# Output projection of heads 0 to 13 by seven block products per pair of heads instead of eight, from batch 2 on

## The reference

```
x = x + attention(layernorm(x))
x = x + ffn(layernorm(x))
# attention, head h:
#   scores = (q_nope k_nope^T + rope(q_pe) rope(k_pe)^T) / sqrt(192);  p = softmax(scores)
#   out   += (p v_h) @ wo_h^T          (512 x 128 times 128 x 512, for each head)
# ffn: silu(x Wg * sg) * (x Wu * su), then @ Wd * sd, weights rounded to fp8
```

## Time and profile before

| | |
|---|---|
| time, median of 3 runs | 2230.44 us (2229.0 to 2231.82) |
| profiled execution, from first to last instruction | 2228.8 us |
| PE busy | 2205.4 us, 10977 matmuls |
| DVE, ACT, POOL busy | 1557.8, 1066.6, 1001.5 us |
| chain that ended last | 93% PE, 3% DVE |
| granted TensorE clock | 0.999 of full speed, mean |
| DMA, all from SP's queue | 218 MB, 47.7% of 16 engines |

### The profile page before, as it was taken

The page is one execution under the profiler, slowest core; times in us unless marked ns, Lnnn a source line. Parts: engine busy times, 40 slices in busy tenths (PEclk is TensorE's granted clock), DMA queues, the critical chain, the costliest instruction groups (busy, mean ns, idle before and its releaser), DMA issues.

```text
span 2228.8 us, 34908 instructions
## 1 busy us (share of the span) xinstructions
PE 2205.4 (99%) x10977; PEld 1026.8 (46%) x10977; DVE 1557.8 (70%) x3227; ACT 1066.6 (48%) x2345; POOL 1001.5 (45%) x688
## 2 busy tenths in 40 slices
PE   7999999999999999999999999999999999999999
PEld 5444544445444454444544445444454445444454
DVE  7888887776477764777648775587755877467773
ACT  6667564554255542555325553355443554345532
POOL 4657465453355524454244642536334363343322
PEclk9999999999999999999999999999999999999999
DMA  7868336562175631756216561365614564145530
GB/s 248 188 124 150 88 71 142 106 124 51 23 151 105 122 53 34 145 105 127 44 43 146 106 121 29 73 123 106 118 25 104 106 115 95 24 104 109 106 65 19
DMA packets 703800, 219.42 MB, mean 98 GB/s; under 512 B 685520, under 2 KB 685776, under 8 KB 702672
## 3 DMA queue, kind: packets, MB, share of 16 engines
q1 hardware_dynamic: 703696, 218.09, 47.7%
HBM read 40.78 MB, written 8.39 MB: 22 GB/s over the span
## 4 chain that ended last, share of the span: by engine, by line
PE 93%; DVE 3%; ACT 1%; DMA 1%; POOL 1%; issue 1%; SPq 0%; DVEq 0%; POOLq 0%
PE bank L853 13%; PE bank L291 11%; PE bank L293 11%; PE bank L292 11%; PE scores L863 7%; PE scores L663 5%; PE scores L293 5%; PE scores L291 5%; PE scores L292 5%; PE bank L674 4%; PE bank L675 4%; PE bank L676 4%; PE scores L660 3%; PE bank L840 1%; PE bank L689 1%; PE scores L557 1%
## 5 line engine op out<-in xcount | busy, mean ns | idle before, releaser
L1716 POOL TENSOR_TENSOR arena<-arena 128x1024 f16<-128x1024 f32 x256 | 545.7, 2132 | 620.3 <-ACT arena L1079 620.3
L1077 ACT ACTIVATE arena<-scores,shift 128x512 f32<-128x512 f32 x512 | 357.5, 698 | 535.0 <-DVE shift L1429 494.8
L1449 DVE SCALAR_TENSOR_TENSOR arena<-bank,rden,arena 128x512 f32<-128x512 f32 x508 | 347.9, 743 | 137.0 <-PE bank L293 137.0
L1427 DVE TENSOR_REDUCE mx<-scores 128x1 f32<-128x512 f32 x512 | 352.5, 689 | 20.5 <-PE scores L293 16.7
L1079 ACT ACTIVATE arena<-scores,shift 128x512 f16<-128x512 f32 x512 | 358.6, 700 | 0.0
L853 PE MATMUL bank<-arena,WFF 128*128 128x512 f16 x1392 | 313.5, 379 | 0.8 <-DVE arena L1601 0.6
L1774 POOL TENSOR_TENSOR arena<-arena 128x512 f16<-128x512 f32 x96 | 114.4, 1191 | 255.6 <-ACT arena L1152 255.6
L853 PEld LDWEIGHTS bank<-arena,WFF 128*128 128x128 f16 x1392 | 135.9, 98 | 164.1 <-DVE arena L1601 2.3
L291 PE MATMUL bank<-WVO,arena 128*128 (+1 forms) x512 | 194.2, 379 | 2.4 <-DVE arena L1222 1.2
L1222 DVE SCALAR_TENSOR_TENSOR arena<-bank,arena 128x512 f16<-128x512 f32 (+1 forms) x263 | 176.2, 670 | 29.1 <-ACT arena L1070 24.4
L663 PE MATMUL scores<-arena 128*128 128x512 f16 x512 | 195.4, 382 | 0.0
(11 more groups left out here) (159 smaller groups left out, 3480.5 us busy)
## 6 DMA issues: line engine op xcount, KB each, us to landing
arena<-arena SPq DMA_TRANSPOSE x712, 3.2
arena<-w_ffn SPq DMA_DIRECT2D x24, 384.0 KB, 3.5
arena<-x SPq DMA_DIRECT2D x8, 1024.0 KB, 5.6
out<-arena SPq DMA_DIRECT2D x32, 256.0 KB, 2.0
arena<-x SPq DMA_DIRECT2D x14, 512.0 KB, 4.4
WVO<-w_o SPq DMA_DIRECT2D x4, 1024.0 KB, 8.2
arena<-w_nope SPq DMA_DIRECT2D x4, 768.0 KB, 9.1
arena<-down_scale SPq DMA_DIRECT2D x8, 256.0 KB, 3.3
```

The source lines that it names most:

```text
L1077: act.activation(P32[:, t, :], SC[:, t, :], ACT.Exp, scale=EXP_SCALE, bias=shift[:, t:t + 1], accum_out=esum[:, par, t:t + 1]).then_inc(s[ ...
L1427: dve.tensor_reduce(mx[:, t:t + 1], SC[:, t, :], AX_X, ALU.max).then_inc(s["mxr"], 1)
L1449: dve.scalar_tensor_tensor(out=XR[:, t, :], in0=banks[t][:, :], scalar=by[:, t:t + 1], in1=XR[:, t, :], op0=ALU.mult, op1=ALU.add).then_in ...
L1716: pool.tensor_tensor(PL[:, par, two, :], P32[:, two, :], PH[:, par, two, :], ALU.subtract).then_inc(s["pl"], 1)
```

## The change

From batch 2 on, the outputs of heads 2j and 2j+1 (j = 0 to 6) are made together. Both contexts side by side are 512 rows by 256, both weights one above the other 256 by 512. Cut in two by two blocks, this product is made with seven block products in place of eight (Winograd's form of Strassen's scheme), from sums and differences of the context's blocks (`E1, O1, O2, S1..S4`) and of the weights' blocks (`B11, B21, B22, T1..T4`). A block product (`duo_product`) is two row tiles x three matmuls of 256 columns. The sums of weights are made once, in batch 1, by POOL and ACT in the place of the weights, and stored to DRAM (`w_duo`); from batch 2 on they are streamed in for each pair, in an early and a late part, into one buffer. The sums of contexts are made on POOL for each pair. Since products mix heads, the context must be scaled by the softmax reciprocal before: a row of 512 reciprocals is written to DRAM and read back broadcast to all partitions, and DVE multiplies the context by it. Heads 14 and 15, and batches 0 and 1, keep the old form. The loops over pairs in PE and ACT are written out in the new batches.

```diff
+EARLY = [(X_E1, W_B11, 0, True), (X_S1, W_T1, 1, True), (X_O1, W_B21, 2, True), (X_S2, W_T2, 0, False)]
+LATE = [(X_S3, W_T3, 0, False), (X_S4, W_B22, 1, False), (X_O2, W_T4, 2, True)]
+ADDS = [(0, 0, 0), (1, 1, 1), (2, 0, 0), (0, 0, 1), (0, 1, 0), (0, 1, 1), (1, 0, 1), (2, 1, 0)]
+        DBANK = (BO, BT, BC)
 # SP
+            def early_blocks(b, j):
+                if j == 0:
+                    sp.wait_ge(s["t_out"], 16 * N_DUO)
+                    sp.wait_ge(s["outp"], b * (NH * NT))
+                else:
+                    sp.wait_ge(s["outp"], b * (NH * NT) + 8 * (j - 1) + N_EARLY)
+                sp.dma_start(WB[:, :, 0:N_EARLY], w_duo[j, :, :, 0:N_EARLY]).then_inc(s["w_early"], 16)
+            def row_of_head(b, i):
+                sp.wait_ge(s["rden"], b * NH + i + 1)
+                sp.dma_start(rows_d[i % 2].rearrange("(t p) -> p t", p=P), rden_duo[:, i % 2],
+                             allow_slow_non_contiguous=True).then_inc(s["row_out"], 16)
+                sp.wait_ge(s["row_out"], (b - B_PLAIN) * (16 * 2 * N_DUO) + 16 * (i + 1))
+                sp.dma_start(ROW[:, i % 2], rows_d[i % 2:i % 2 + 1].broadcast_to((P, S))).then_inc(row_in[i % 2], 16)
...
                     head(i, base, i % 2, ahead=i < NH - 2, first=first)
+                    if not plain:
+                        if i < 2 * N_DUO:
+                            row_of_head(b, i)
+                        if i == 0:
+                            early_blocks(b, 0)
+                            late_blocks(b, 0)
+                        elif i >= 4 and i % 2 == 0:
+                            early_blocks(b, i // 2 - 1)
+                        elif i >= 5:
+                            late_blocks(b, i // 2 - 1)
...
 # PE
+            def duo_product(j, x, w, k, start):
+                for t in range(2):
+                    dst = DBANK[k][:, t * HB:(t + 1) * HB]
+                    for m, (p, q) in enumerate(((0, 0), (0, 1), (1, 0))):
+                        r = pe.matmul(dst, lhsT=XP[j % 2][:, p, x, tile(t)], rhs=WB[:, q, w, :],
+                                      start=(start and t == 0 and m == 0), stop=(m == 2), skip_group_check=True)
+            def duo_early(b, j):
+                n, base = (b - B_PLAIN) * N_DUO + j + 1, b * (NH * NT) + 8 * j
+                pe.wait_ge(s["w_early"], 16 * n)
...
+                    if x == X_S1:
+                        pe.wait_ge(s["x_lo"], n)
+                    if x == X_O1:
+                        pe.wait_ge(s["cth"], b * N_CT + min(2 * j + 3, 2 * N_DUO))
+                    if x == X_S2:
+                        pe.wait_ge(s["outr"], base + 1)
+                    duo_product(j, x, w, bk, start).then_inc(s["outp"], 1)
+            def duo_step(b, i, ahead=True):
+                scores(b, pair, par)
+                values(b, *before(pair, par))
+                if ahead:
+                    absorb(i + 2, b * NH + i + 2)
+                if i >= 3 and i % 2:
+                    duo_early(b, (i - 3) // 2)
+                elif i >= 4:
+                    duo_late(b, (i - 4) // 2)
 # ACT
+            def sum_hi(j):                     # batch 1, 128 x 1024
+            def context_hi(b, i):
+                act.wait_ge(s["cth"], b * N_CT + i + 1)
...
+            def duo_step(b, i):
+                probs(b * NH + i, i % 2, False)
+                context_hi(b, i - 1)
+                qa_hi(b * NH + i + 2, i % 2)
 # DVE
+            def duo_step(b, i, part=None):
+                maxima(g)
+                if part in (0, 1, 2):
+                    next_norm(b, part)
+                context_by_row(b, i - 1)
+                row_of_sums(b, i)
+                qa_lo(g + 2, i % 2)
+                context_lo(b, i - 1)
+                if part in (2, 3):
+                    next_norm(b, part + 1)
+                duo_adds(b, i)
 # POOL: block_sums in batch 1: ten tensor_tensor of 128 x 256; block_sums_lo: one of 128 x 1024
+            def context_sums(b, j):
+                step(x[X_S1], x[X_S3], x[X_O2], ALU.add, 0)
+                step(x[X_S3], x[X_E1], x[X_S3], ALU.subtract, 1)
+                step(x[X_S2], x[X_S1], x[X_E1], ALU.subtract, 0)
+                step(x[X_S4], x[X_O1], x[X_S2], ALU.subtract, 3)
+                pool.tensor_copy(XP[j % 2][:, 0, X_S3:], X32[:, X_S3:]).then_inc(s["x_sum"], 1)
+                pool.tensor_tensor(XP[j % 2][:, 1, X_S3:], X32[:, X_S3:], XP[j % 2][:, 0, X_S3:],
+                                   ALU.subtract).then_inc(s["x_lo"], 1)
...
                     head(base + i, i % 2)
+                    if not plain and i >= 2 and i % 2 == 0:
+                        context_sums(b, i // 2 - 1)
+                    if plain and not first and i >= 2:
+                        if i % 2 == 0:
+                            block_sums(i // 2 - 1)
+                        else:
+                            block_sums_lo(i // 2 - 1)
```

More of the change, by code:

```diff
@@ L464, in batch @@
                         weight_chunk(chunk_of(i) + 2)
+                if plain and not first:
+                    sums_of_blocks(N_DUO - 1)
                 sp.wait_ge(s["ctp"], (b + 1) * N_CT)
@@ L511, in _ @@
             output_matrix(3)
-            batch(0, False, first=True)
-            with sp.Fori(1, B - 1) as b:
+            batch(0, False, first=True, plain=True)
+            batch(1, False, plain=True)
+            with sp.Fori(B_PLAIN, B - 1) as b:
                 batch(b, False)
@@ L776, in attention @@
                     rotated_ahead(b, n)
-                head_step(b, 0, 1)
-                if first:
+                if b >= B_PLAIN:
+                    for i in range(1, NH - 2):
+                        duo_step(b, i)
+                else:
+                    head_step(b, 0, 1)
+                if b >= B_PLAIN:
+                    pass
+                elif first:
                     for i in range(2, NH - 2):
@@ L1112, in attention @@
                         head_step(i, base, i % 2, chunk=chunk_of(i), weights=True)
-                else:
[L1114 to L1117, removed]
+                elif plain:
+                    for i in range(2, NH - 2):
+                        head_step(i, base, i % 2)
+                        if i >= 3 and i % 2:
+                            sum_hi((i - 3) // 2)
+                else:
+                    for i in range(2, NH - 2):
+                        duo_step(b, i)
                 for k in range(2):
@@ L1181, in ffn, with batch @@
                     qa_hi((b + 1) * NH + 1, 1)
-            def batch(b, last, first=False):
-                attention(b, last, first)
+            def batch(b, last, first=False, plain=False):
+                attention(b, last, first, plain)
                 ffn(b, last, first)
@@ L1212, in _ @@
             setup_queries_and_keys()
-            batch(0, False, first=True)
-            with act.Fori(1, B - 1) as b:
+            batch(0, False, first=True, plain=True)
+            batch(1, False, plain=True)
+            with act.Fori(B_PLAIN, B - 1) as b:
                 batch(b, False)
@@ L1565, in last_of_attention @@
                 maxima(g)
-                for t in range(NT):
+                if b >= B_PLAIN:
+                    duo_adds(b, NH - 1)
+                for t in range(NT if b < B_PLAIN else 0):
                     add_out(g - 2, t)
@@ L1746, in attention @@
+            def attention(b, last, first, plain):
                 base = b * NH
@@ L1802, in _ @@
             rotate(0, NT)
-            batch(0, False, first=True)
-            with pool.Fori(1, B - 1) as b:
+            batch(0, False, first=True, plain=True)
+            batch(1, False, plain=True)
+            with pool.Fori(B_PLAIN, B - 1) as b:
                 batch(b, False)
```

218 lines of the change are left out of this document (200 added, 18 removed).

## The result

The changed kernel takes 3054.0 us (median; 3051.4 to 3055.0) against 2231.1 of the kernel before (2229.0 to 2234.5) on the same chip: ratio 1.3685, 95% interval 1.3666 to 1.3704. The forecast was 2294, range 2250 to 2350. The direction was right, the time is far outside the range.

A forecast was written before the change was run, and what follows sets the result against it. It took TensorE, 99% busy and 93% of the last-ending chain, as the bound. Batches 2 to 6 lose 10.0 each (50), batch 7 6.1, batch 1 8: +64 on 2230.4 gives 2294, range 2250 to 2350.

The forecast's parts named there:

- The row of reciprocals: Each head's write to DRAM and broadcast back from SP: write lands in 2.6, costing nothing at 2.0 to 3.7.
- the rows' round trip is the bound: Rival: chain from SP over two DMAs to PE bounds, from a write of about 3.7 us; 2385 at 5; chance 0.25.
- 256-wide products: PE: 42 matmuls of 256 columns per pair at 0.109 replace 24 of 512; saves 0.58 per pair, 24.4 us in all.
- wait for DVE's first add: PE's fourth early product waits for DVE's first add: 0.7 in first pair, then 1.5 a pair, 8.2 per batch.
- DVE's low halves of the context: DVE's low context half ahead of the adds: 0.7 in the even step, 0.42 in the odd step.
- weights' place: Early weights on SP's queue land near +8.7 of the odd step; up to 1.3 later costs nothing.
- POOL, batches 2 to 6: POOL's context sums and normalisation make it 3.6 late at step 9, PE waits 1.3, later weaker: 2 per batch.
- batch 1: POOL's sums of weights delay step 11's subtractions, so values wait for transposes: charged 8 us.
- everything but the rows: Sum of all terms, with the row at nothing: 64 us over the kernel before.
- The term of 2 per batch for the short steps: Steps 1 and 2 are 8.6 long; transposes land 1 us late behind queued weights and residual: 2 per batch.
- the POOL rival: POOL's 256-wide ops cost 0.85 or more; its items grow 2 in batch 1, 1 in later ones: 2304; chance 0.03.
- I am wrong: Sign: the fourth product's wait is under 0.6, or rows or weights, not adds, end PE's waits.

The follow-up runs named there:

- (2): Changed kernel with no reciprocals written or read back, contexts of heads 0 to 13 multiplied by ones from batch 2 on: 2406.2 us, ratio 1.0791.
- (1): Changed kernel with reciprocals written in 128 runs of 16 bytes, not 512 elements of 4, and DVE reading the row with a stride: 2486.3 us, ratio 1.1153.
- (9): As (8), but the row written in 128 runs of 16 bytes instead of single elements: 2423.0 us, ratio 1.0858.
- (7): 6 with scaling and high half of the next input moved from POOL to ACT in batches 2 to 6: 2335.3 us, ratio 1.0461.
- (10): (7) with neither write nor read back of reciprocals, contexts multiplied by ones: 2265.3 us, ratio 1.0148.
- (8): Changed kernel still writing single elements per head, nobody waiting soon, nothing read back, contexts multiplied by ones: 2805.6 us, ratio 1.2568.
- (4): (2) with DVE's four adds ahead of the low halves of query and context: 2345.3 us, ratio 1.0515.
- 5: (1) with each half of a pair's weights issued ahead of the next head's transposes, the first pair's at the previous batch's end: 2414.5 us, ratio 1.0820.
- 6: (1) with DVE's adds first, weights placed as in 5, and the write issued between a head's transposes: 2355.2 us, ratio 1.0549.

## Why the prediction was wrong

**The term that failed** is "The row of reciprocals": "With 2.6 for the write (nearer to the store ...)", "So nothing at 2.0 to 3.7". The write took 9.0, and with it the row cost 648 ((2) against the kernel after) where nothing was forecast. Runs (1) and (9) settle what made it slow: the same bytes in 16-byte runs land in 2.1. But "nothing at 2.0 to 3.7" fails as well: (1), with a write of 2.1, is still 80 slower than (2), and (7) 70 slower than (10). The broadcast lands in 4.3 there, not in 3.3, and 33 us of DVE's time come from the strided reading that (1) brought in. I bounded the write by rows whose runs are long, a store in rows and a load of 16 bytes per partition, and took 6.5 for the upper end. What differs, and has no row before, is that the row is written in 512 separate pieces instead of 128. Pieces of 16 bytes are no slower than a store in rows (2.1 and 2.0); whether it is the number of pieces or their 4 bytes that costs was not parted. The Trainium skill (DMA: Bandwidth & Descriptors, Rules for kernel authors), cited in the prediction, says that a strided last dimension is one descriptor per element; the trace agrees, 384 packets more for each write. It should have set the upper end: four times the store's 2.0 is up to 8, an estimate, and 9.0 was measured.

**The rival "the rows' round trip is the bound"** (the third in the list, though the term of the row calls it the second) was the mechanism: its chain and its queue. The write of 84 heads is 25% of the chain that ended last, 762 us, which is 84 x 9.0: every one of them stands on it. I gave the rival 0.25 and 2385. Its price was a delay of the dependent chain, 1.3 a pair at 5 us. By its own numbers the write of 9.0 would be 5.3 beyond the deciding point per pair, 191 in 36 pairs, and as much again for SP's issues, 380 in all; against a write of 2.1 it was 568. Three things are missing in it. It counts a pair, but every head has its trip, and each is passed on whole: 84 x 6.9 = 580. The write also delays the transfers behind it: 383 stay when no one waits ((8) less (9)), so the blocking wait is the smaller part. And PE's clock falls behind gaps, some 33 us a batch.

**The other terms.** Except for batch 1 they can't be read in the kernel after, as the row hides them:

| step | forecast | measured |
|---|---|---|
| 256-wide products | 0.109 each | 18 in 2.13 against 6 in 0.83 (2): 0.108 |
| wait for DVE's first add | 49 in all | 63.9 (2); 61 gained by (4) |
| DVE's low halves of the context | 0.7 and 0.42 | 1.17 and 1.18 (2) |
| weights' place | 0 | 72 (5 against 1) |
| POOL, batches 2 to 6 | 10 | 20 for the normalisation alone (7 against 6) |
| PE's lower clock | 0 | some 59 (2), an estimate |
| batch 1 | 8 | 10.2 (after), 8.5 (2) |
| everything but the rows | 64 | 175 (2) |

That the add's wait is larger than forecast may come from the low halves of the context, which stand ahead of the adds; no run tests it. The one of the odd steps took not 0.42 but 1.1 where it stood beside POOL's subtraction. DVE's row, then POOL's, of such a place:

```profile
1292.15 1.11 DVE L1658 TENSOR_TENSOR WVO<-WVO 128x256 f16<-128x256 f32 x1
```

```profile
1290.87 2.12 POOL L1983 TENSOR_TENSOR arena<-arena 128x1024 f16<-128x1024 f32 x1 [0.36 <-ACT arena L1227]
```

**The weights at nothing.** I followed pairs one to six, where the wait for the add covers a late landing, and gave the last pair and the batch's start no wait or 2. There nothing covers it: in batch 4 of (2) the last pair waits 1.22 + 5.37, the first values 3.61, and behind those PE runs at the lower clock for some 5.5 us. The term of 2 per batch for the short steps had the right place and half the size, and the last pair's wait and the clock had no term. The sum of the POOL rival is also off: 2 in batch 1 and 1 in each later one are at most 8, not 10, which changes nothing here.

**What would show it**, as listed: the wait of 1.5 at the fourth product appears in (2) (1.8 each), not in the kernel after; PE's busy time was to fall by 25 and rose by 173; the write was to land in 2 to 3.7. The sign for "I am wrong", that rows or weights end PE's waits, is what the profile after shows.

## What to carry to other kernels

Count the pieces of a transfer, not only its bytes, and where no row has pieces as small, let the upper bound grow with their number. A slow transfer also holds up those queued behind it that need nothing from it; here that was more (383 us) than the wait for it. A saving of 1% (24.4 of 2231) on an engine that is 99% busy is soon lost to gaps: behind one of 3.6 us PE also ran 5.5 us at its lower level, so price the start and the end of a batch as carefully as its middle.

## What I had not expected of the hardware

- A write of 2 KB in 512 pieces of 4 bytes landed in 9.0 us (7.8 to 10.8), in 128 pieces of 16 bytes in 2.1. 512 KB queued behind the first landed in 12.6 (8), behind the second in 5.1 (9).
- DVE's subtraction of 128x256 from SBUF to SBUF took 0.41 with POOL idle (after) and 1.18 on average in (2), where a subtraction of POOL lies beside most of them (34 of 42, at 0.65 to 2.12; the other 8 took 0.41); the product of a bank and the row (0.69) did not change. The Trainium skill (GPSIMD Engine Reference, Specifications) names contention between the two engines for DVE instructions with two inputs in SBUF; the rows agree, as the subtraction has two and the product one.
- Behind the gap of 3.6 us in (2), PE's 512-wide matmuls started every 0.43 us instead of 0.215, for about 5.5 us (granted clock 0.50).
- DVE's product of context and row took 0.69 with the row read in order and 1.08 with a stride of four elements.
